# First half of the routing done inside cross attention, expert stage opened by a shared unit

## What is computed

```python
x = x + self_attention(layernorm(x))                   # 16 heads, causal
x = x + cross_attention(layernorm(x), ctx)             # 16 heads, 375 context rows per batch
x = x + moe(layernorm(x))

# moe, xt = all 896 tokens
scores = sigmoid(xt @ gate.T)                          # 8 experts
_, sel = top_k(scores + expert_bias, 2)
routed = xt[token] * score[token, chosen]              # each token twice, to bf16
h  = silu(routed @ w1[e].T) * (routed @ w3[e].T)       # e = the expert chosen for that row
out_r = h @ w2[e].T
hs = silu(xt @ shared_w1.T) * (xt @ shared_w3.T)       # shared expert, all tokens
out = hs @ shared_w2.T;  out[token] += out_r
```

## Time and profile before

| | us |
|---|---|
| runs of the kernel | 628.71, 629.47, 630.12 (median 629.47) |
| the profiled execution's own time | 630.01 |
| its span | 628.2 |
| PE, DVE, ACT, POOL busy | 565.0, 387.5, 291.1, 296.1 |
| mean granted clock of TensorE | 0.944 |

### The profile page before, as it was taken

The page is one execution under the profiler, slowest core; times in us unless marked ns, Lnnn a source line. Parts: engine busy times, 40 slices in busy tenths (PEclk is TensorE's granted clock), DMA queues, the critical chain, the costliest instruction groups (busy, mean ns, idle before and its releaser), DMA issues. The chain is left out here.

```text
span 628.2 us, 9692 instructions
## 1 busy us (share of the span) xinstructions
PE 565.0 (90%) x3435; PEld 446.0 (71%) x3440; DVE 387.5 (62%) x916; ACT 291.1 (46%) x660; POOL 296.1 (47%) x290
## 2 busy tenths in 40 slices
PE   2858898998988969999999999999999967999995
PEld 1535575676666758888988888888888857974553
DVE  6564577677576485646666366564656537856752
ACT  3123451541744557644776357663676513224420
POOL 0507734542662436631785228860387400555631
PEclk9978898998998979999999999999999995699998
DMA  8853565465925036612633346242420009279535
GB/s 275 217 197 75 195 220 179 118 226 182 300 89 162 29 109 182 159 34 77 172 86 83 83 127 173 38 74 59 168 68 2 0 1 347 106 161 209 171 105 151
DMA packets 52979, 85.00 MB, mean 135 GB/s; under 512 B 25699, under 2 KB 34613, under 8 KB 52037
## 3 DMA queue, kind: packets, MB, share of 16 engines
q1 hardware_dynamic: 49540, 71.55, 36.6%
q0 software_dynamic: 2656, 11.91, 8.3%
q10 hardware_dynamic: 736, 0.92, 0.5%
HBM read 63.20 MB, written 30.09 MB: 148 GB/s over the span
## 5 line engine op out<-in xcount | busy, mean ns | idle before, releaser
L1448 POOL TENSOR_TENSOR xprob<-xprob,erec 128x375 f32<-128x375 f32 x112 | 90.4, 815 | 136.1 <-DVE erec L1227 135.8
L915 ACT ACTIVATE xprob<-s_ps,nmax 128x375 f32<-128x375 f32 x112 | 64.3, 575 | 59.7 <-DVE nmax L1222 56.9
L1222 DVE TENSOR_REDUCE nmax<-s_ps 128x1 f32<-128x375 f32 x112 | 59.7, 538 | 0.0
L59 PE MATMUL k_ps<-ow,ctx_hl 128*112 128x512 f32 x128 | 52.5, 410 | 2.8 <-DVE ctx_hl L1217 2.2
L1441 POOL TENSOR_TENSOR prob<-prob,rec 112x1792 f32<-112x1792 f32 x8 | 25.5, 3188 | 54.8 <-DVE rec L1163 54.8
L1217 DVE TENSOR_TENSOR ctx_hl<-k_ps,ctx_hl 128x448 fp32r<-128x448 f32 x32 | 20.0, 625 | 50.6 <-ACT ctx_hl L910 50.6
L61 PE MATMUL k_ps<-ow,ctx_hl 128*112 128x512 f32 x128 | 50.5, 394 | 0.0
L60 PE MATMUL k_ps<-ow,ctx_hl 128*112 128x512 f32 x128 | 50.2, 392 | 0.0
L1197 DVE TENSOR_TENSOR pt_hl<-f_ps,pt_hl 125x512 fp32r<-125x512 f32 (+1 forms) x67 | 41.7, 624 | 11.1 <-ACT pt_hl L887 10.3
L59 PE MATMUL s_ps<-kvt,qt_hl 128*128 128x376 f32 x112 | 44.9, 401 | 2.0 <-ACT xprob L915 1.0
L887 ACT CAST pt_hl<-f_ps 125x512 fp32r<-125x512 f32 (+1 forms) x67 | 35.7, 534 | 14.1 <-PE f_ps L645 13.7
(11 more groups left out here) (243 smaller groups left out, 1530.6 us busy)
## 6 DMA issues: line engine op xcount, KB each, us to landing
ow_raw<-ow_dram SPq DMA_DIRECT2D x16, 512.0 KB, 3.6
w<-w_dram SPq DMA_DIRECT2D x6, 1024.0 KB, 10.9
raw_b<-in_raw SPq DMA_DIRECT2D x8, 640.0 KB, 5.2
raw_m<-in_raw SPq DMA_DIRECT2D x8, 576.0 KB, 4.8
raw_q<-in_raw SPq DMA_DIRECT2D x8, 512.0 KB, 6.4
ow_dram<-bw_sb SPq DMA_DIRECT2D x8, 512.0 KB, 5.8
qw_raw<-aw_dram SPq DMA_DIRECT2D x16, 256.0 KB, 3.6
w_dram<-in_w POOLq DMA_DIRECT2D x8, 512.0 KB, 5.5
```

Of the source, the lines that this page charges most:

```text
L59: pe.matmul(out, a_hl[0], b_hl[0], start=start, stop=False, skip_group_check=True)
L915: act.activation(xprob[z][:, 0:L], s_bank(n, k)[:, 0:L], ACT.Exp, bias=nmax[:, z:z + 1], accum_out=esum[:, z:z + 1]).then_inc(xexp_done, 1)
L1222: dve.tensor_reduce(nmax[:, z:z + 1], s_bank(n, k)[:, 0:L], X, ALU.max, negate=True).then_inc(xmax_done, 1)
L1448: pool.tensor_tensor(xprob[z][:, 0:L], xprob[z][:, 0:L], erec[:, z:z + 1].broadcast_to([128, L]), ALU.mult).then_inc(xp_ready, 1)
```

## The change

The routing of batches 0 to 3 (half 0) moves out of the expert stage into steps 9 to 16 of cross attention. DVE makes their 1/sqrt in steps 9 and 10 (`norm_seed`, `norm_steps`) and normalises one batch at a time into `xn0`. PE turns them (T0 to T3) and multiplies by `gate` (G0 to G3) at two places of steps 10, 11 and 13, and counts (C) in step 14. These nine are uses of the three turning banks, so `ring` grows by them. Choice, slots and rows of half 0 come on DVE from step 13 to step 16. POOL scatters the rows of half 0 behind its last normalisation. The scores get 9 buffers in place of 10, which makes room for the new tiles. `gate`, `bias` and `iota` are loaded early, the mask's triangle is taken from self attention's mask.

The expert stage has only half 1 left to normalise, turn, route and scatter. PE opens with `shared_unit(0)`, which needs only batches 0 to 3, and the turning, routing and counting of half 1 stand between the four units. SP opens with the turning DMA of the first seven blocks, ahead of the six weight loads. `owners(1)` stands behind the last shared unit's low part.

```diff
+def norm_seed(dve, own, stats_all, norm, bs):
+
+    mean, rstd, vv, newt = norm
+    dve.wait_ge(own.sem, own.base + own.n)
+    for b in range(bs.start, bs.stop):
+        dve.bn_aggr(mean[:, b, :], stats_all[:, b, :]).then_inc(own.sem, 1)
+    own.n += bs.stop - bs.start
+    dve.wait_ge(own.sem, own.base + own.n)
+    v, y, t = vv[:, bs], rstd[:, bs], newt[:, bs]
+    own.link(dve.tensor_copy(v, mean[:, bs, 1]))
+    rsqrt_seed(dve, own.link, v, y, t, y.bitcast(I32), t.bitcast(I32), v.bitcast(I32))
+
+
+def norm_steps(dve, own, norm, bs):
+    rsqrt_steps(dve, own.link, norm[2][:, bs], norm[1][:, bs], norm[3][:, bs])
+
...
+def pick(dve, own, r, bias):
+
+    own.link(dve.reciprocal(r.score[:, :, :], r.score[:, :, :]))
+    own.link(dve.tensor_tensor(r.ranked[:, :, :], r.score[:, :, :], bias[:, :].unsqueeze(1).broadcast_to([T, HALF, EXPERTS]), ALU.add))
+    for s in range(HALF):
+        dve.max(r.best[:, s, :], r.ranked[:, s, :]).then_inc(own.sem, 1)
+    own.n += HALF
+    dve.wait_ge(own.sem, own.base + own.n)
...
+def mark(dve, own, r, iota, both_ready):
+
+    own.link(dve.tensor_copy(r.whichf[:, :, :], r.which[:, :, 0:TOP2]))
+    for t in range(TOP2):
+        dve.tensor_tensor(r.chosen[:, t], iota[:, :].unsqueeze(1).broadcast_to([T, HALF, EXPERTS]),
+                          r.whichf[:, :, t:t + 1].broadcast_to([T, HALF, EXPERTS]), ALU.is_equal).then_inc(own.sem, 1)
...
-    SLOTS = 10
+    SLOTS = 9
...
+    ROUTED = 2 * HALF
+    INSIDE = {ROUTED + 2: ("T0",), ROUTED + 3: ("G1", "T2"), ROUTED + 5: ("G3",), ROUTED + 6: ("C",)}
+    BEHIND = {ROUTED + 2: ("G0", "T1"), ROUTED + 3: ("G2", "T3")}
+    AT = {name: n for part in (INSIDE, BEHIND) for n, names in part.items() for name in names}
+
     def ring(n):
-        return FIRST if n == 0 else STARTS if n % HALF == 0 and n < STEPS else LATER
+        if n == 0 or (n % HALF == 0 and n < STEPS):
+            return FIRST if n == 0 else STARTS
+        return LATER[0:4] + INSIDE.get(n, ()) + LATER[4:] + BEHIND.get(n, ())
 
...
+            def turn_tokens(b):
+                n, name = AT[f"T{b}"], f"T{b}"
+                pe.wait_ge(xn0_ready, b + 1)
+                turn(x_take(n, name), xn0, filled)
+            def route_tokens(b):
+                n, name = AT[f"G{b}"], f"G{b}"
+                pe.wait_ge(high_copied, use(AT[f"T{b}"], f"T{b}") + 1)
+                bank = x_take(n, name)
+                if b == 0:
+                    pe.wait_ge(rows_laid, 16 * 7)
+                for k in range(KC):
+                    mm = pe.matmul(bank[0:T, 0:EXPERTS], xt0[:, k, :], gate[:, k, :], start=(k == 0), stop=(k == KC - 1))
+                mm.then_inc(filled, 1)
+            def count_chosen():
+                pe.wait_ge(both_ready, 1)
+                count_rows(pe, x_take(AT["C"], "C"), route, tri, ones).then_inc(filled, 1)
...
@@ -718,6 +900,7 @@
                 x_scores(n, 4)
                 gather(n, 0)
                 x_project(n - 2, 3)
+                route_part(INSIDE.get(n, ()))
...
                 x_project(n - 1, 0)
                 x_project(n - 1, 1)
                 gather(n, 1)
+                route_part(BEHIND.get(n, ()))
...
+            def tokens_high(b):
+                name = f"T{b}"
+                n = AT[name]
+                act.wait_ge(filled, use(n, name) + 1)
+                act.copy(xt0[:, :, :], cols(bank_of(n, name)))
+                act.copy(x2_part(0, b), cols(bank_of(n, name))).then_inc(high_copied, 1)
...
+            def tokens_normal(b):
+
+                name = f"T{b - 1}"
+                if b:
+                    dve.wait_ge(filled, use(AT[name], name) + 1)
+                else:
+                    dve.wait_ge(rows_laid, 16 * 7)
+                dve.tensor_scalar(xn0[:, :], x_sb[:, b, :], norm[0][:, b, 0:1], norm[1][:, b:b + 1],
+                                  ALU.subtract, ALU.mult).then_inc(xn0_ready, 1)
...
+            def lay_rows(b):
+
+                if b == 0:
+                    dve.wait_ge(filled, use(AT["T3"], "T3") + 1)
+                else:
+                    dve.wait_ge(rows0_ready, TOP2 * b)
+                own.link(dve.tensor_scalar(xn0[:, :], x_sb[:, b, :], norm[0][:, b, 0:1], norm[1][:, b:b + 1],
+                                           ALU.subtract, ALU.mult))
+                if b >= 2:
+                    dve.wait_ge(sent0[b % 2], 16 * TOP2)
+                for r in range(TOP2):
+                    dve.tensor_scalar(rows0[b % 2][:, r, 0:C], xn0[:, :], route.weight[:, r, b:b + 1], None,
+            def early_part(n):
+
+                if n == ROUTED + 2:
+                    norm_steps(dve, own, norm, FIRST_HALF)
+                    tokens_normal(0)
+                if n == ROUTED + 3:
+                    tokens_normal(2)
+                if n == ROUTED + 6:
+                    mark(dve, own, route, iota, both_ready)
+                if n == ROUTED + 7:
+                    lay_rows(0)
+
+            def late_part(n):
+
+                if n == ROUTED + 1:
+                    norm_seed(dve, own, stats_all, norm, FIRST_HALF)
+                    dve.wait_ge(rows_laid, 16 * 7)
+                    own.link(dve.tensor_tensor(below[:, :, :], iota[:, :].unsqueeze(1).broadcast_to([T, EXPERTS, EXPERTS]),
+                                               iota[:, :].unsqueeze(2).broadcast_to([T, EXPERTS, EXPERTS]), ALU.is_lt))
+                if n == ROUTED + 2:
+                    tokens_normal(1)
+                if n == ROUTED + 3:
+                    tokens_normal(3)
+                if n == ROUTED + 5:
+                    dve.wait_ge(emptied, use(AT["G3"], "G3") + 1)
+                    pick(dve, own, route, bias)
+                if n == ROUTED + 6:
+                    weigh(dve, own, route)
+                    dve.wait_ge(emptied, use(AT["C"], "C") + 1)
+                    locate(dve, own, route, below, counts0[:, 0:HALF * EXPERTS], slot0_ready)
+                if n == ROUTED + 7:
+                    lay_rows(1)
+
             def start_step(n):
                 pair_low(n, 0)
                 probs_low(n, "A", 0)
...
                 probs_low(n, "B", 1)
                 norm_stats(n - 2)
                 probs_low(n, "B", 2)
+                lay_rows(2)
+                lay_rows(3)
                 x_context_low(n, 1)
...
+            def send_rows(s):
+
+                z = s % 2
+                rows_u = rows0[z][:, :, :].bitcast(I32)
+                if s < 2:
+                    pool.wait_ge(emptied, use(AT["G3"], "G3") + 1)
+                    own.link(pool.memset(rows_u[:, :, C // 2 + 1:ROW // 2], 0))
+                else:
+                    pool.wait_ge(sent0[z], 16 * TOP2)
+                own.link(pool.tensor_copy(rows_u[:, :, C // 2:C // 2 + 1], token[:, :, s:s + 1]))
+                if s == 0:
+                    pool.wait_ge(slot0_ready, 1)
+                    pool.wait_ge(rows_laid, 16 * 7)
+                for r in range(TOP2):
+                    pool.wait_ge(rows0_ready, TOP2 * s + r + 1)
+                    pool.indirect_dma_start(slots_dram[0], bass.IndirectOffsetOnAxis(ap=route.slot_u[:, r, s:s + 1], axis=0),
+                                            rows0[z][:, r, :], None).then_inc(sent0[z], 16)
 
...
+                def turn_slots(h, z):
+                    j = slice(z * CHUNK * 128, (z + 1) * CHUNK * 128)
+                    sp.dma_start_transpose(xg[CHUNKS * h + z][:, :, :], slots_dram[h][j, 0:C]).then_inc(xg_loaded, 16)
+
+                def load_places(h):
+                    rows_of = slots_dram[h].rearrange("(j p) c -> p j c", p=128)
+                    sp.dma_start(to[:, h], rows_of[:, :, C:ROW].bitcast(I32)).then_inc(to_loaded[h], 16)
+
+                for z in range(2):
+                    sp.wait_ge(sent0[z], 16 * TOP2 * (HALF // 2))
+                turn_slots(0, 0)
                 sp.wait_ge(w_cast, 16 * (EXPERTS + 2))
                 for e in range(0, EXPERTS, 2):
                     sp.dma_start(w13[:, e:e + 2], w13_dram[e:e + 2].rearrange("e p w k n -> p e w k n")).then_inc(w_loaded, 16)
                 for e in range(0, EXPERTS, 4):
                     sp.dma_start(w2[:, e:e + 4], w2_dram[:, e:e + 4]).then_inc(w_loaded, 16)
-
-                def load_slots(h):
-                    sp.wait_ge(sent[h], 16 * TOP2 * HALF)
-                    if h:
...
-                for b in range(HALF):
-                    turn_tokens(b)
-                pe.wait_ge(small_loaded, 64)
-                route(0)
-                for b in range(HALF, B):
-                    turn_tokens(b)
-                count(0)
-                route(1)
                 shared_unit(0)
-                count(1)
+                for s in range(HALF):
+                    turn_tokens(s)
                 shared_unit(1)
+                route_tokens()
                 shared_unit(2)
+                count_chosen()
                 shared_unit(3)
...
```

(58 more changed lines are left out.)

443 lines of the change are left out of this document (249 added, 194 removed).

## The result

The changed kernel takes 635.39 us (median of 4 runs, 633.43 to 636.65) against 629.72 us before (4 runs in the same session). The ratio is 1.0108, with a 95% interval of 1.0083 to 1.0133. The forecast was 621.3, range 617.0 to 627.0: it was wrong in sign. The profiled execution has a span of 634.3 us, 6.1 above the 628.2 of before.

A forecast was written before the change was run, and what follows sets the result against it. The prediction took PE to bound cross attention and 48.97 us to precede the expert stage's first turned hidden rows. Gain 17.4, less 5.7 added PE work, 1.0 stalls and 2.5 clock, gave 8.2 us: forecast 621.3 us, range 617.0 to 627.0.

The forecast's parts named there:

- What bounds the kernel: Cross attention PE-bound; expert stage spends 48.97 us before the first turned hidden rows, with a DVE wait and half clock.
- Expert stage, S+31.6: First `turn_hidden(0)` comes 31.6 us after S, the expert stage's start, against 48.97 before: 17.4 us gained.
- Weights: Expert stage: weight loads delayed by SP's turning DMA land by S+28.6 at the latest and cost nothing.
- Clock lost in the pause: PE stands five microseconds before `turn_hidden(0)`, so first blocks run at 1.2 GHz: 2.5 us lost, bounds 0 and 3.5.
- PE's added work, 5.7: Cross attention: four turnings, four gates and one count lengthen full PE by 5.7 us (4.7 to 6.6).
- Stalls by DVE's insertions, 1 us with bounds 0 and 5: Cross attention: DVE's insertions mostly fit its 1.6 us waits before each `ctx_hl`; overruns cost 1 us in all.
- The bound of 5 us: Upper bound on cross attention stalls from DVE's insertions: nine bank uses, each 0.55 us late.
- Rival C: POOL's scatters are held up beside DVE's work in cross attention's last step: 2.6 us worse, 623.9; chance 0.05.
- Rival D: Insertions stall PE in cross attention through three turning banks, 1.5 us per added use: 633.8 us; chance 0.06.
- Rival B: Clock also lost at the block change into the expert stage, slowing units 0 and 1: 2.0 us worse, 623.3; chance 0.12.

The follow-up runs named there:

- a_moved: Changed kernel, expert stage untouched, half 0's cross attention work moved beside POOL's idle time (steps 12, 13, 15, last): 625.24 us against 629.26 before, ratio 0.9943.
- a_both: a_moved plus `owners(1)` and low parts of shared units 1 to 3 behind the first blocks' hidden rows: 621.20 us against 629.26 before, ratio 0.9884.
- experiment 1: POOL's low parts of later cross attention and shared weights zeroed by memset: changed kernel 627.58 us, kernel before 633.62, both against 633.89 (ratios 0.9896, 1.000).
- b_recip: Kernel before plus five dependent small SBUF reciprocals on DVE ahead of each `ctx_hl` in six steps: 636.27 us against 634.45, ratio 1.0019.
- a_best: Changed kernel, half 0's routing in step 12, marks ending step 13, `owners(1)` and low parts behind first blocks' hidden rows: 630.81 us against 634.45 before, ratio 0.9955.

## Why the prediction was wrong, point by point

- **What bounds the kernel**: right. The wait for `fxn`, the half clock over transposes and gates, and DVE's chain ahead of the blocks were the 49 us, and most of them went.
- **Expert stage, S+31.6**: 33.11 measured; the 1.5 above it is the clock lost at the block change. In a_moved, where it was kept, 31.55. The chain of links was priced link by link from rows of the same place, with POOL issuing only scatters beside it.
- **Weights** hidden: right, PE's `up(0)` waited for nothing at S+26.3. **Clock lost in the pause**: right, 64.36 - 61.79 = 2.57 against 2.5.
- **PE's added work, 5.7** (4.7 to 6.6): right within a microsecond. By themselves the added products take 4.9: the eight gate products of a batch 0.71 until the next product starts (424.60 to 425.31) against 0.9, a turning about 0.4, the count 0.43. What is left of cross attention's lengthening without standing and half clock is 6.5 (a_both) to 6.9 (the changed kernel, 19.4 - 12.5). The difference of 1.6 to 2.0 lies in neighbouring products that take a little longer; it wasn't taken apart.
- **Stalls by DVE's insertions, 1 us with bounds 0 and 5**: this is the step that failed. Measured: 9.1 us of standing and 3.4 of half clock behind it, 12.5 us. I priced each inserted instruction by rows from the expert stage, where POOL is idle or issues DMAs, and carried these durations to steps 9 to 16, where POOL is busy half of the time (one of its 2.37 us subtractions). The sum of busy times was compared with DVE's idle time, and nobody asked what POOL ran meanwhile. Of the 12.5 us, POOL's long instructions make at least 9 (experiment 1), with the clock lost behind the pauses they cause among them; the banks, small hand-overs and what is still held beside the shorter memsets make the rest. The sign was in the profile of the kernel before, in self attention (98.65, above).
- **The bound of 5 us** was "nine uses, each 0.55 late". It was no bound at all: a single four-number instruction could be late by 2.7.
- **Rival C** was the right kind of thing the wrong way round. I read the 3.35 us scatter as POOL held by DVE and priced only that direction. The scatters of half 0 in the last step all took 0.94 to 1.05, so it cost nothing here.
- **Rival D** gave 633.8, near the 635.4. That its time came out near was mostly luck: its mechanism (banks emptied late, 1.5 us each) is there only in part, some 2 us of PE's waits in a_both. Its sign, waits of over 1 us at `ctx_hl`, did appear (2.35 us before 517). And 0.06 was far too little for it: the evidence against it was the 1.6 us of cover, which is what failed.
- **Rival B** came true in five of the eight profiles with a shared unit first, and cost 1.6 us (33.11 against 31.55, and 29.41 against 27.85) where 2.0 was forecast.

## What to carry to other kernels

Before small DVE work moves to another stage, look at what POOL does there, not only at DVE's idle time: a copy of four numbers costs what is left of POOL's current instruction. Put such work where POOL waits, or pick forms that aren't held, and price it by rows from a place with the same neighbours. A duration many times that of the same shape elsewhere is a wait, though the page counts it as busy.

## What the runs showed of the hardware

- One-input DVE instructions from SBUF to SBUF (copies, casts, `tensor_scalar`) stood while POOL ran a multiplication, an addition, a subtraction or a memset, or issued a cast DMA: 0.17 us became up to 2.87. Beside POOL's issue of a scatter they were not held for long (casts and copies of `owners` 0.16 us, rows at most 0.2 longer), so the rows of the expert stage showed next to nothing. Two-input ones with both inputs in SBUF stood beside subtractions (0.63 became 1.81) and multiplications (`L93` of step 10, 0.16 became 0.81) but not beside a memset (0.63, one case). Not held were instructions with an input in PSUM (`ctx_hl` 0.60 to 0.63), reciprocals (0.16 to 0.18 in b_recip), `tensor_reduce` and `max8` (0.15 to 0.17). The Trainium skill, page "SBUF — State Buffer", section "SBUF: two separate sides", says just this: the port pair that DVE and GpSimd share is locked for a whole instruction by a DVE instruction in a mode that uses two ports, or by one with two SBUF inputs, the latter only against a GpSimd instruction that reads SBUF. The rows named here agree with it. I had used that section for one direction only.
- The normalisation with two scalars per partition is held as well, and holds POOL in its turn. In the kernel after it began at 413.44, 0.14 us before the first of two multiplications of POOL ended, and took its normal 0.53; the second of them took 1.03 us instead of 0.81. In a_moved it began 0.45 us before the end of such a multiplication (510.31) and took 0.80. The same came out in a_best and a_both.

```profile
412.77 1.86 POOL L1747 TENSOR_TENSOR xprob<-xprob,erec 128x375 f32<-128x375 f32 x2 [3.66 <-DVE erec L1437]
...
413.44 0.53 DVE L1460 TENSOR_SCALAR r_xn<-x_sb,mean,rstd 112x512 f32<-112x512 f32 x1
```

```profile
508.68 1.64 POOL L1820 TENSOR_TENSOR xprob<-xprob,erec 128x375 f32<-128x375 f32 x2 [2.88 <-DVE erec L1485]
...
509.86 0.80 DVE L1542 TENSOR_SCALAR r_xn<-x_sb,mean,rstd 112x512 f32<-112x512 f32 x1
```

- The clock behind a pause of PE of 2 us at the block change was 0.50 in five profiles and 1.00 in three (a_best, a_moved, a_both), with the same pause of 2.0 us. What decides isn't known. The eight differ in what PE did in the 21 us ahead of it: the five had one more pause of 1.14 to 2.35 us there, the three one of 0.58, besides the 0.67 and 1.37 us that all eight have. The row of a_moved that answers to 538 to 540 above:

```profile
532.00:534.00 2.00, 2.00 (x12) 1.85 (x11) 1.69 (x10) 0.00 (x0) 0.00 (x0) 1.00 1.19 235
```
